# Summing the last inversion products on TensorE, and splitting one GpSimd product, in a gated-recurrence plus mixture-of-experts kernel

## The reference, cut to what matters

```python
def step(S, inp):
    g, a_t, b_t, k_t, v_t, q_t = inp
    bS = jnp.einsum('bhk,bhkv->bhv', b_t, S)
    S = jnp.exp(g)[..., None] * S + a_t[..., None] * bS[:, :, None, :] + k_t[..., None] * v_t[:, :, None, :]
    o = jnp.einsum('bhk,bhkv->bhv', q_t, S)
    return (S, o)
```

## Time and profile before

| | us |
|---|---|
| median of 3 runs | 1971.96 |
| lowest, highest | 1968.42, 1979.21 |
| the profiled execution: its time | 1968.42 |
| its span in the trace | 1966.6 |

### The profile page before, as it was taken

The page is one execution under the profiler, slowest core; times in us unless marked ns, Lnnn a source line. Parts: engine busy times, 40 slices in busy tenths (PEclk is TensorE's granted clock), DMA queues, the critical chain, the costliest instruction groups (busy, mean ns, idle before and its releaser), DMA issues. The chain is left out here.

```text
span 1966.6 us, 68546 instructions
## 1 busy us (share of the span) xinstructions
PE 1525.7 (78%) x26124; PEld 1291.1 (66%) x26125; DVE 1165.4 (59%) x3492; ACT 780.1 (40%) x1805; POOL 755.4 (38%) x912
## 2 busy tenths in 40 slices
PE   5499999998656478555886647776577799999995
PEld 5499999997235365343753525545365799999994
DVE  7546444443287777767777696767956346444442
ACT  1243333332466235562345643356433243333331
POOL 2555322222075251572413725228344123522221
PEclk9999999999778598786687967878757899999998
DMA  9553322222101000010000001000100653333224
GB/s 302 182 158 86 73 48 48 48 48 38 54 7 47 22 21 22 6 46 25 22 22 4 24 27 38 17 10 12 41 12 11 217 161 60 84 68 49 47 48 109
DMA packets 84242, 116.31 MB, mean 59 GB/s; under 512 B 12952, under 2 KB 74464, under 8 KB 82016
## 3 DMA queue, kind: packets, MB, share of 16 engines
q1 hardware_dynamic: 56224, 76.27, 12.2%
q0 software_dynamic: 27360, 37.80, 10.7%
q10 hardware_dynamic: 544, 0.86, 0.1%
HBM read 64.87 MB, written 54.21 MB: 61 GB/s over the span
## 5 line engine op out<-in xcount | busy, mean ns | idle before, releaser
L1059 POOL DMA_INDIRECT x<-ffn_yout,ffn_place x142 | 222.2, 1565 | 532.3 <-DVE ffn_yout L991 449.0
L997 DVE TENSOR_TENSOR ffn_inner<-ffn_inner,ffn_bank 128x512 f32<-128x512 f32 x142 | 97.5, 687 | 354.7 <-PE ffn_bank L871 352.3
L871 PE MATMUL ffn_bank<-ffn_tileT,ffn_gate_now 128*128 128x128 f32 x2272 | 280.2, 277 | 0.0
L871 PE MATMUL ffn_bank<-ffn_tileT,ffn_up_now 128*128 128x128 f32 x2272 | 278.3, 276 | 0.0
L881 PE MATMUL ffn_bank<-ffn_w,ffn_inner 128*128 x1136 | 268.9, 380 | 1.7 <-DVE ffn_yout L991 1.7
L871 PEld LDWEIGHTS ffn_bank<-ffn_tileT,ffn_gate_now 128*128 128x128 f32 x2272 | 268.4, 194 | 0.1
L952 ACT ACTIVATE ffn_inner<-ffn_bank 128x512 f32<-128x512 f32 x142 | 84.8, 597 | 459.9 <-PE ffn_bank L871 459.8
L871 PEld LDWEIGHTS ffn_bank<-ffn_tileT,ffn_up_now 128*128 128x128 f32 x2272 | 266.7, 193 | 0.0
L881 PEld LDWEIGHTS ffn_bank<-ffn_w,ffn_inner 128*128 128x128 f32 x1136 | 205.0, 190 | 24.4 <-issue 2.5
L814 ACT COPY ffn_gate_now<-ffn_w 128x1024 f32 x142 | 148.4, 1045 | 29.1 <-issue 21.9
L814 DVE COPY ffn_up_now<-ffn_w 128x1024 f32 x142 | 98.9, 696 | 52.6 <-issue 42.4
(11 more groups left out here) (493 smaller groups left out, 3114.0 us busy)
## 6 DMA issues: line engine op xcount, KB each, us to landing
ffn_w<-in_w1t_dram SPq DMA_DIRECT2D x16, 1024.0 KB, 5.4
ffn_tile<-xs SPq DMA_DIRECT2D x122, 130.0 KB, 2.1
ffn_w<-in_w2t_dram SPq DMA_DIRECT2D x16, 512.0 KB, 6.5
ffn_x<-in_x_dram SPq DMA_DIRECT2D x16, 256.0 KB, 5.8
x<-ffn_x SPq DMA_DIRECT2D x16, 256.0 KB, 5.7
pass_xa<-x SPq DMA_DIRECT2D x12, 256.0 KB, 3.2
pass_xr<-x SPq DMA_DIRECT2D x12, 256.0 KB, 2.6
x<-pass_xr SPq DMA_DIRECT2D x12, 256.0 KB, 2.2
```

Source lines behind the costliest of these rows:

```text
L871: t = pe.matmul(bank[:, i * P:(i + 1) * P], half_now[half][b][:, k, i * P:(i + 1) * P], rowsT[b][:, k * P:(k + 1) * P], start=(k == 0), st ...
L997: dve.tensor_tensor(inner[b][:, :], inner[b][:, :], p_u[b][:, :], ALU.mult).then_inc(s_act, 1)
L1059: pool.indirect_dma_start(total, bass.IndirectOffsetOnAxis(ap=place[b][:, 0:1], axis=0), yout[b][:, :], None, compute_op=ALU.add).then_inc ...
```

## The change

Part one, in `decays_and_triangles`: the product of 512 columns becomes two of 256, one for each `s`. Operands and results are the same numbers.

```diff
-                        pool.tensor_tensor(out[:, :, 8:12].rearrange("p n (a s) -> p n a s", s=2), planes([[0, 2]]),
-                                           late2.unsqueeze(3).to_broadcast([P, NB, 2, 2]), ALU.mult).then_inc(s_pr, 1)
+                        for s, first in ((0, kf2), (1, two(k, c))):
+                            i = pool.tensor_tensor(out[:, :, 8:12].rearrange("p n (a s) -> p n a s", s=2)[:, :, :, s],
+                                                   first[:, :, 0:1].to_broadcast([P, NB, 2]), late2, ALU.mult)
+                        i.then_inc(s_pr, 1)
```

```diff
+    TERMS = (0, 1, 2, 3, 5, 7, 9, 11, 15, 13)
+    FORMED = (1, 2, 3, 7, 10, 13, 16, 19, 21, 22)
+    ring = [pr[:, i, :] for i in range(3)] + [zz[:, :]] + [...]   # three more in a_top
...
+        eng.wait_ge(s_ev, GROUPS)
+        for p, one, two in ((0, zterm, zpair), (1, xterm, xpair)):
+            if p > 0:
+                eng.wait_ge(s_acc, PARTS)
+            for x in range(CT):
+                if 7 <= x <= 10:
+                    eng.wait_ge(s_acc, PARTS * p + x - 6)
+                elif x in (12, 14):
+                    eng.wait_ge(s_acc, PARTS * p + x // 2 - 1)
+                step(one(x))
+                if x in (5, 7, 9, 11, 13):
+                    step(two(x - 2))
+            step(two(CT - 3))
...
+            def total(p, y):
+                x = TERMS[y]
+                pe.wait_ge(s_inv, SMALL + PRODUCT * p + FORMED[y])
+                if p == 0:
+                    for half in range(2):
+                        heads = slice(half * HQ // 2, (half + 1) * HQ // 2)
+                        t = pe.matmul(z_sum[:, heads, :, 0:CT - x], ident[:, :], term(x)[:, heads, :, 0:CT - x],
+                                      start=(y == 0), stop=(y == PARTS - 1), skip_group_check=True)
+                else:
+                    H = CT // 2
+                    if x < H:
+                        pe.matmul(x_sum[0][:, :, x:H, :], ident[:, :], term(x)[:, :, 0:H - x, :], ...)
+                    first = max(x, H)
+                    t = pe.matmul(x_sum[1][:, :, first - H:H, :], ident[:, :], term(x)[:, :, first - x:CT - x, :], ...)
+                t.then_inc(s_acc, 1)
```

More of the change, by code:

```diff
@@ L1880, in invert, with term, back_bank @@
     SIZES = (2, 4, 8, 16)
-    LAST = 2 * (2 * CT - 1)
-    STEPS = sum(2 * (2 * m - 1) for m in SIZES)
+    SMALL = sum(2 * (2 * m - 1) for m in SIZES[:-1])
+    TERMS = (0, 1, 2, 3, 5, 7, 9, 11, 15, 13)
+    FORMED = (1, 2, 3, 7, 10, 13, 16, 19, 21, 22)
+    PRODUCT, PARTS = FORMED[-1], len(TERMS)
+    ring = [pr[:, i, :] for i in range(3)] + [zz[:, :]] + [
+        a_top[:, :, :].rearrange("p g x -> p (g x)")[:, i * HQ * CT * CT:(i + 1) * HQ * CT * CT] for i in range(3)]
+    def term(x):
+        return ring[x % len(ring)].rearrange("p (b j i) -> p b j i", b=HQ, j=CT)
+    z_sum = env["wide"][:, :].rearrange("p (b j i) -> p b j i", b=HQ, j=CT)
+    x_sum = [psum[i][:, :].rearrange("p (b j i) -> p b j i", b=HQ, j=CT // 2) for i in range(2)]
+    def back_bank(n):
+        return psum[n] if n < 8 else psum[4 + n % 4]
     def square(t):
@@ L1929, in step @@
                 eng.wait_ge(s_inv, n[0] - 1)
-        for size, m in enumerate(SIZES):
+        for size, m in enumerate(SIZES[:-1]):
             if size == 0:
@@ L1985, in inverse, with blk, zterm, xterm @@
             product(xmult, xadd)
-        assert n[0] == STEPS
+        assert n[0] == SMALL
+        def blk(t, j0, nj, i0, ni, dj=SUB, di=1):
+            return bass.AP(tensor=t, offset=j0 * SUB + i0, ap=[[HQ * HS, P], [SUB * (SUB + 1), HQ], [dj, nj], [di, ni]])
+        def zterm(x):
+            kk = CT - 1 - x
+            return eng.tensor_tensor(term(x)[:, :, :, 0:kk + 1], blk(ng, CT, CT, kk, kk + 1, di=0), blk(tm, kk, CT, 0, kk + 1, dj=0), ALU.mult)
+        def xterm(x):
+            rows = CT - x
+            return eng.tensor_tensor(term(x)[:, :, 0:rows, :], blk(tm, CT + x, rows, CT + x, CT, di=0), z_sum[:, :, x:x + 1, :].to_broadcast([P, HQ, rows, CT]), ALU.mult)
+        def zpair(x):
+            a, b = term(x)[:, :, :, 0:CT - 1 - x], term(x + 1)[:, :, :, 0:CT - 1 - x]
+            return eng.tensor_tensor(a, a, b, ALU.add)
+        def xpair(x):
+            a, b = term(x)[:, :, 1:CT - x, :], term(x + 1)[:, :, 0:CT - 1 - x, :]
+            return eng.tensor_tensor(a, a, b, ALU.add)
+        eng.wait_ge(s_ev, GROUPS)
[11 more added lines that the diff above has]
+            step(two(CT - 3))
+        assert n[0] == SMALL + 2 * PRODUCT
     with nc.Block() as block:
@@ L2002, in _, with back @@
                 t.then_inc(s_tp, 1)
[L2004 to L2024, removed]
+            def back(n):
@@ L2025, in _ @@
                 if n >= 8:
-                    pe.wait_ge(s_bke, n - 7)
+                    pe.wait_ge(s_bke, n - 3)
                 for cc in range(4):
                     src = aq[:, 4 * n + cc, :, :] if n < 4 else tc[:, 4 * (n - 4) + cc, :, :]
-                    t = pe.transpose(psum[n % 8][:, cc * P:(cc + 1) * P], src.rearrange("p h i -> p (h i)"), ident[:, :])
+                    t = pe.transpose(back_bank(n)[:, cc * P:(cc + 1) * P], src.rearrange("p h i -> p (h i)"), ident[:, :])
                 t.then_inc(s_bk, 1)
+            def total(p, y):
[9 more added lines that the diff above has]
+                    if x < H:
+                        pe.matmul(x_sum[0][:, :, x:H, :], ident[:, :], term(x)[:, :, 0:H - x, :],
+                                  start=(y == 0), stop=(x == H - 1), skip_group_check=True)
+                    first = max(x, H)
+                    t = pe.matmul(x_sum[1][:, :, first - H:H, :], ident[:, :], term(x)[:, :, first - x:CT - x, :],
+                                  start=(y == 0), stop=(y == PARTS - 1), skip_group_check=True)
+                t.then_inc(s_acc, 1)
@@ new lines, in _ @@
+            pe.wait_ge(s_ev, GROUPS)
+            pe.wait_ge(s_aq, 3)
+            for n in range(4):
+                back(n)
+            for j, (t, g, c) in enumerate(VALUES):
+                if j < 4:
+                    pe.wait_ge(s_bke, j + 1)
+                    for kc in range(KCH):
+                        t = pe.matmul(psum[j][:, :], wv[:, kc, g * P:(g + 1) * P], xT[:, kc, c * 512:(c + 1) * 512],
+                                      start=(kc == 0), stop=(kc == KCH - 1))
+                else:
+                    pe.wait_ge(s_vale, j - 3)
+                    t = pe.matmul(psum[j % 4][:, :], wrank[RANK:2 * RANK, g * P:(g + 1) * P], fg[RANK:2 * RANK, c * 512:(c + 1) * 512], start=True, stop=True)
+                t.then_inc(s_val, 1)
@@ new lines, in _ @@
+            pe.wait_ge(s_vale, len(VALUES))
+            for p in range(2):
+                for y in range(PARTS):
+                    total(p, y)
+                    if (p, y) == (0, 3):
+                        pe.wait_ge(s_tc, 2)
+                        back(4)
+                    elif (p, y) == (0, 5):
+                        back(5)
+                    elif (p, y) == (1, 2):
+                        back(6)
+                    elif (p, y) == (1, 4):
+                        back(7)
+                    elif (p, y) == (1, 6):
+                        pe.wait_ge(s_tc, 3)
+                        back(8)
+                    elif (p, y) == (1, 7):
+                        back(9)
@@ L2065, in _, with compact, back @@
                 i.then_inc(s_ev, 1)
[L2067 to L2087, removed]
+            def compact(rows, cols, src=None):
+                src = tmv[:, :, rows, cols] if src is None else src
+                act.copy(tc[:, rows, :, cols], src.rearrange("p h j i -> p j h i")).then_inc(s_tc, 1)
+            def back(n):
                 act.wait_ge(s_bk, n + 1)
@@ L2090, in _ @@
                 act.copy(ta[:, :, :, col:col + 4].rearrange("p u c j -> p c u j"),
-                         psum[n % 8][:, :].rearrange("p (j c u) -> p c u j", j=4, c=CHAINS)).then_inc(s_bke, 1)
+                         back_bank(n)[:, :].rearrange("p (j c u) -> p c u j", j=4, c=CHAINS)).then_inc(s_bke, 1)
+            for n in range(4):
+                back(n)
+            act.preload_act_table_set("silu_and_others")
+            for j, (t, g, c) in enumerate(VALUES):
+                act.wait_ge(s_val, j + 1)
+                if j < 4:
+                    act.activation(both(t, g, c), psum[j][:, :], ACT.Silu).then_inc(s_vale, 1)
+                else:
+                    act.activation(both(t, g, c), psum[j % 4][:, :], ACT.Tanh, scale=0.5).then_inc(s_vale, 1)
+            act.wait_ge(s_inv, SMALL)
+            compact(slice(0, CT), slice(0, SUB))
+            compact(slice(CT, SUB), slice(CT, SUB))
+            for n in range(4, 8):
+                back(n)
+            act.wait_ge(s_acc, PARTS + TERMS.index(CT // 2 - 1) + 1)
+            compact(slice(CT, CT + CT // 2), slice(0, CT), x_sum[0])
+            for n in range(8, 10):
+                back(n)
+            act.wait_ge(s_acc, 2 * PARTS)
```

(3 more changed lines are left out.)

5 lines of the change are left out of this document (4 added, 1 removed).

## The result

| | before | after |
|---|---|---|
| median (lowest to highest), us | 1974.03 (1968.42 to 1979.21) | 2009.78 (2004.64 to 2010.75) |
| the profiled execution: time, span | 1968.42, 1966.6 | 2010.11, 2008.3 |
| mean granted clock | 0.863 | 0.880 |

Both medians are of four runs; those of before are the three above and one more. The ratio is 1.0176 with the interval 1.0142 to 1.0211, so the change made the kernel slower by 1.8%. I had forecast no change, 1967 us.

A forecast was written before the change was run, and what follows sets the result against it. GpSimd was taken to set the decays, VectorE plus a 3.3 us tail the inversion. The terms -8.3 + 5.6 - 0.5 = -3.2 us gave 1965.2 on the profiled execution, 1968.8 on the median; forecast 1967, range 1957 to 1977.

The forecast's parts named there:

- GpSimd's pair: Decays: two 256-column products replace one of 512, 1.67 us a pair, saving 0.26 a chain, 8.3 us in all.
- rival 3: Decays: GpSimd's pair isn't cheaper, as the slow rate belongs to the columns; 17.7 us above the sum, 1985; chance 0.11.
- The step that failed: Inversion's last size: TensorE is free for VALUES at 625.5, after group 3's transposes, so VALUES end at 637.3.
- The sum for an undisturbed last size: Inversion's last size, to ScalarE's last copy: 1.4 us a pass more than the 42.4 before.
- The stall before the eighth multiplication: Inversion's last size: VectorE stands still some 6 us, waiting for the first total behind all VALUES.
- The 2 us of low clock: Inversion's last size: TensorE's sums run their first 4 us or so at 1.2 GHz, losing 2 us.
- The bounds that I gave beside the sum: Inversion, a pass: -1.1 us with the full clock throughout, +31 us with 1.2 GHz throughout.
- my 5.6 us of loss in four passes: Inversion: TensorE's sums and a longer tail cost 1.4 us a pass, 5.6 us for four.
- wrong altogether: Sign of failure: inversion's last size, to ScalarE's last copy, takes less than 41 or more than 46 us.
- (1): Scan: TensorE's clock stays up from the sums into the scans; 30 us less, 1937; chance 0.12.
- (2): Inversion: sums come early enough for VectorE's full saving; -46 and -8.3 us, some 1914; chance 0.05.
- (4): Inversion: TensorE's clock stays at 1.2 GHz through one product; about 10 us a pass slower, 2007; chance 0.08.

The follow-up runs named there:

- second_sums: Kernel before plus GpSimd's edit, scatters held behind ScalarE's copies, TensorE summing only the second product: 1930.24 us, ratio 0.9841; repeated 1948.52, 0.9856.
- pool_hold: Kernel before plus GpSimd's edit, its 16 scatters held until ScalarE has copied all 18 groups, no TensorE sums: 1962.49 us, ratio 0.9907.
- values_between: Kernel after with held scatters, TensorE's VALUES moved between the first and second product's totals: 1975.47 us, ratio 1.0001 to the kernel before.

## Why the prediction was wrong

**GpSimd's pair: right, and a little better.** Forecast 1.67 us a pair, measured 798 ns x 2 less their overlap, 1.55 in the timeline, plus the wait; chains start 5.70 us apart where it was 6.00. That is 9.6 us for 32 chains of the 12 to 13 that the stage lost, against 8.3. The rest lies behind GpSimd's last product. A half with `late2`'s jump takes 798 ns, the packed L1725 735, so rival 3 is refuted. The Trainium skill's rule on reads with a long step (GPSIMD Engine Reference, Performance pitfalls for Q7 kernels: about half more) doesn't show here, where it is 9%.

**The step that failed** is "TensorE is free for them when the transposes of group 3 end, 623.59 + 1.91 = 625.5", and with it the unspoken one that the last size starts where it started. Both rest on ScalarE's copies of the 18 groups. In the kernel after, group 3's transposes end at 638.77 + 1.91 = 640.7, 3.6 us behind the last size's start where I had 0.1, and that start is itself 5.3 us late in this pass. I listed the new wait for all 18 groups in the change and gave it no price; the rows showed ScalarE's copies on time, so it seemed free. That was one execution. In the second profile of the same kernel VALUES, which follow the copies, end 8.6 to 10.7 us later against the last size's start, and nothing on the path waits for them. Of the 41.5 us lost in the inversion, holding the scatters gave back 24.0 ahead of the last size and 14.5 in it (187.26 to 172.79): 38.5, the 39 of the ratios.

**The sum for an undisturbed last size was sound.** Forecast 43.8 us a pass; with held scatters it took 43.1 to 43.4. The stall before the eighth multiplication was 8.4 us for 6, the first product 25.7 for 25.6, the second with its tail 17.4 for 18.2. The 2 us of low clock that I had put on the first product's end fall on its first total, for which VectorE waits; with them my stall would have been some 8. The bounds that I gave beside the sum don't add up: by their own terms they are -0.6 and +21 us a pass, not -1.1 and +31. Nothing else rested on them. Even my 5.6 us of loss in four passes stands beside 3.0 measured. My statement that I am "wrong altogether" above 46 us holds for the kernel after: 47.09, 46.40, 46.77 and 47.00.

**The rivals.** (1) The clock was up to the end of the last size, but the scans ran at mean clocks of 0.75, 0.82, 0.67 and 0.73, as before: refuted. (2) VectorE's saving in full: refuted by 11.41 us of idle time; with half of the summing it came to 4.7 us a pass in second_sums (151.0 us for four last sizes against 169.8). (3) is refuted above. (4) The clock was low for 4 us, not for a product: its time of 2007 was near the result by luck, its mechanism didn't occur. What I lacked was a rival in which the late event is another engine's, ahead of the changed code.

**Open.** Why the copies are delayed in some executions and not in others. Of 14 profiles seven had holes in the copies of `aq`: just those with the first decay product late (559.0 to 563.6) and the scatters free to overlap the copies. Four had it late (560.4 to 563.9) and the scatters held, and no holes. Three had it early (551.4 to 552.9) and no holes, two of them with free scatters. So the scatters are one condition and something else, which comes with the late start, is another. The experiments of one job were all of the same kind in this. I didn't try a kernel without the scatters, or one in which another queue carries them.

## What to carry to other kernels

An engine with slack can be late by more in one execution than in another without anyone seeing it: before you hang a wait on it, take two profiles and see how late it can be, not how late it was. When work moves to an engine, add up all that this engine must do from the event that frees it to the event that is needed; if that takes longer than the work that the other engine has left, reordering only moves the stall, and moving half of the work can win where moving all of it gains nothing. And where something on the path waits for copies, a burst of scatters with no deadline is worth starting behind them: one wait was worth some 39 us here, and nothing by the trace in pool_hold, where the path doesn't wait for them.

## What the runs showed of the hardware

ScalarE's ten copies of `aq` in a pass (276 to 294 ns in the mean) follow one another within 0.03 us. In seven profiles in which GpSimd issued indirect scatters beside them (1.3 to 1.6 us apart in the kernel after), they stood up to 3.4 us apart (2.6 in the rows above). In two profiles with such scatters, and in all five with held ones, they didn't. One GpSimd product of 512 columns in which both operands jump took 1846 ns, two of 256 columns each with one operand repeated took 798 each, 14% less. Of TensorE's clock: the first 4 us of totals behind the VALUES ran at a granted clock of 0.50 in the first pass of the kernel after, and in two passes of values_between at 1.00.
